# Two feed-forward blocks exchange places in a pipelined macaron kernel, with a ring of three residual buffers and a token-major beta

## What is computed

```
x = x + 0.5 * FFN(layernorm(x))          # FFN: gelu(h @ w1 + b1) @ w2 + b2, 256 -> 1024 -> 256
x = x + ATTN(layernorm(x))
x = x + 0.5 * FFN(layernorm(x))

ATTN(x): q, k, v = silu(conv4(x @ W))    # 4 heads of 64
         beta = sigmoid(x @ Wb)          # one number per token and head
         q, k = l2norm(q), l2norm(k)
         delta = delta_rule(q, k, v*beta, k*beta, chunks of 32)   # T = (I - A)^-1 per chunk
         branches = fir3(v), fir31(v), delta, v
         w = softmax(gelu([x, stats, branches] @ gW1 + gb1) @ gW2 + gb2), floored, renormalised
         return rmsnorm(sum(w * branches)) @ Wo
```

## Time and profile before

| | us |
|---|---|
| median of 3 executions (1224.04, 1224.04, 1238.88) | 1224.04 |
| the profiled execution | 1227.37 |
| its span, from the first to the last instruction | 1225.7 |
| PE busy in it | 1056.4 (86%) |
| DVE busy | 820.9 (67%) |
| ACT busy | 549.3 (45%) |
| POOL busy | 415.6 (34%) |
| mean granted TensorE clock | 0.932 of full |

### The profile page before, as it was taken

One profiled execution on the slowest core, in us unless ns is written; L12 is line 12 of the kernel. 1 busy time (PEld: TensorE's weight loads), 2 busy tenths in 40 slices (PEclk: granted clock), 3 DMA queues, 4 the chain that ended last, 5 costly groups with the idle time before them and its releaser, 6 DMA issues.

```text
span 1225.7 us, 25639 instructions
## 1 busy us (share of the span) xinstructions
PE 1056.4 (86%) x10348; PEld 784.7 (64%) x10348; DVE 820.9 (67%) x1556; ACT 549.3 (45%) x965; POOL 415.6 (34%) x648
## 2 busy tenths in 40 slices
PE   3778598899988999899988996999988998887838
PEld 2654485378745886488736884478736885477427
DVE  5774267785687767875788666875787667863263
ACT  1154236443374337543475336453475337532322
POOL 7106500671019500681028400681028400870000
PEclk9889699899999999989999999999999999995668
DMA  5040104110040203111040203011040204020000
GB/s 153 1 102 21 34 1 97 25 31 22 18 104 1 53 1 94 28 26 27 19 104 1 52 19 86 18 24 30 18 104 1 52 1 96 9 52 1 1 0 18
DMA packets 82293, 47.45 MB, mean 39 GB/s; under 512 B 57856, under 2 KB 75776, under 8 KB 82176
## 3 DMA queue, kind: packets, MB, share of 16 engines
q1 hardware_dynamic: 82176, 45.82, 16.4%
HBM read 31.12 MB, written 14.68 MB: 37 GB/s over the span
## 4 chain that ended last, share of the span: by engine, by line
PE 57%; DVE 22%; ACT 8%; issue 5%; SPq 3%; POOL 3%; DMA 1%; DVEq 0%; ACTq 0%; POOLq 0%
PE psum L782 12%; PE psum L784 10%; PE psum L783 10%; DVE conv_acc L1363 4%; PE psum L813 4%; DVE arena L1594 3%; PE psum L975 3%; PE psum L960 3%; PE psum L994 2%; PE psum L999 2%; SPq L347 2%; PE psum L1152 2%; ACT arena L582 2%; DVE arena L1596 2%; POOL arena L522 1%
## 5 line engine op out<-in xcount | busy, mean ns | idle before, releaser
L518 POOL TENSOR_TENSOR l_prod<-arena 64x30 f32<-64x30 f32 (+14 forms) x240 | 150.8, 628 | 599.2 <-DMA arena<-l_dram 581.0
L578 ACT ACTIVATE h_f<-psum,b_col 128x512 f32<-128x512 f32 x128 | 88.0, 688 | 216.4 <-PE psum L784 206.4
L522 POOL TENSOR_TENSOR arena<-arena,l_prod 64x30 f32<-64x30 f32 (+14 forms) x240 | 157.3, 655 | 18.8
L782 PE MATMUL psum<-w_hi,h_hi 128*128 128x256 f32 x512 | 152.0, 297 | 9.2 <-DVE h_lo L1343 9.2
L784 PE MATMUL psum<-w_hi,h_lo 128*128 128x256 f32 x512 | 145.2, 284 | 0.0
L783 PE MATMUL psum<-w_lo,h_hi 128*128 128x256 f32 x512 | 145.1, 283 | 0.0
L1081 PE MATMUL psum<-v_shift,fir_w 128*32 128x512 f32 x1152 | 133.6, 604 | 3.6 <-DMA v_shift<-v_dram 3.6
L1363 DVE SCALAR_TENSOR_TENSOR conv_acc<-psum,conv_col,conv_acc 128x511 f32<-128x511 f32 x144 | 107.8, 748 | 33.5 <-ACT conv_acc L603 22.4
L782 PE MATMUL psum<-xt_hi,w_hi 128*128 128x512 f32 x256 | 109.4, 427 | 14.3 <-DVE b_half L1456 7.0
L1342 DVE CAST h_hi<-h_f 128x512 fp32r<-128x512 f32 x128 | 65.3, 510 | 76.6 <-ACT h_f L578 40.1
L782 PEld LDWEIGHTS psum<-w_hi,h_hi 128*128 128x128 f32 x512 | 98.1, 192 | 15.3 <-DVE h_lo L1343 11.1
(11 more groups left out here) (232 smaller groups left out, 2205.6 us busy)
## 6 DMA issues: line engine op xcount, KB each, us to landing
x_in<-in_L_attn_x SPq DMA_DIRECT2D x8, 512.0 KB, 4.0
v_dram<-v_fm SPq DMA_DIRECT2D x8, 512.0 KB, 2.8
v_shift<-v_dram SPq DMA_DIRECT2D x8, 512.0 KB, 5.0
out<-x_tok SPq DMA_DIRECT2D x8, 512.0 KB, 2.9
v_shift<-v_dram SPq DMA_DIRECT2D x8, 511.0 KB, 7.0
v_shift<-v_dram SPq DMA_DIRECT2D x8, 510.0 KB, 9.1
v_shift<-v_dram SPq DMA_DIRECT2D x8, 509.0 KB, 11.6
arena<-in_L_ffn_w SPq DMA_DIRECT2D x2, 1024.0 KB, 7.1
```

The lines of the kernel that those rows point to most:

```text
L518: pool.tensor_tensor(prod, l_inv[:, k + 1:, k:k + 1].broadcast_to(shape), l_inv[:, k:k + 1, 0:k].broadcast_to(shape), ALU.mult).then_inc(i ...
L522: pool.tensor_tensor(l_inv[:, k + 1:, 0:k], l_inv[:, k + 1:, 0:k], prod, ALU.add).then_inc(inverted, 1)
L578: act.activation(h_f[:, m % 2, :], bank, ACT.Gelu, bias=b1_col[:, m:m + 1]).then_inc(read, 1)
L782: pe.matmul(dst, a_hi, b_hi, start=first, stop=False, **kw)
```

## The change

The wide place now runs the *first* FFN of sequence j + 1 ("upw", "outw"), and the filling place runs the *second* FFN of sequence i - 1 ("upr", "outr"). So sequence 0 still has its first FFN alone at the start; head has sequence 1's first FFN behind its front; a new pass "zero" (i = 0) has a back and a front and a wide FFN, but nothing to fill its merge and recurrence; five bodies have both; last (i = 6) fills with sequence 5's second FFN and has no wide FFN; tail fills with sequence 6's second FFN and ends with sequence 7's in the wide place. There are 16 FFNs before and after.

- Layer norm 1 of sequence j + 1 has its statistics ahead of Wo and is normalised between the two halves of Wo's reading on DVE; it is turned ("ln1") behind f_t. The first products of the wide FFN wait for each half of it apart.
- Layer norm 3 of sequence i has its statistics taken behind Wo as before, but is normalised after the fourth split of the wide FFN and turned as "next" near its end, for the filling FFN of the next pass.
- The statistics of layer norm 2 are taken at the end of a pass, behind the residual of the wide FFN, and no longer behind the recurrence.
- Rows live in x_ring, three buffers by sequence modulo 3. The copy on POOL (L499) is gone; the residuals are added in place. SP stores the output of i - 1 and then loads x of i + 2 at the start of a pass; x of sequence 1 is loaded among the weights at the start.
- at0 stands behind the first four steps of the wide FFN, and DVE masks lhalf ahead of the first split.
- beta is made by token: for each of 4 tiles and 2 halves, three products with the 128x128 block of rows as weights and 4 moving columns; ACT takes the sigmoid of 16 columns straight into rows_tok. beta_turn and the copy on DVE are gone.
- Banks: f_t moves from (0, 1, 6, 4) to (0, 1, 7, 2).

```diff
-        x_in = sb("x_in", [P, TILES, C])
-        x1_tok = sb("x1_tok", [P, TILES, C])
-        x2_tok = sb("x2_tok", [P, TILES, C])
+        x_ring = [sb(f"x_ring{n}", [P, TILES, C]) for n in range(3)]
...
+        V_T = [("v_t", (3, 5)), ("f_t", (0, 1, 7, 2))]
+        FFN_W = [("upw", (0, 4) * (KT // 2)), ("outw", (1, 6))]
...
+        front = [LN2, V, K, FIR, Q, V_T, LN1, HALF, FFN_W, L_OFF]
+        both = [STATS, LN2, V, STAT, K, LOGIT, FIR, Q, MIX, V_T]
+        ORDER = {"head": sum(front, first),
+                 "zero": sum([MERGE, RECUR] + both + [LN1, HALF, FFN_W, L_OFF, NEXT], []),
+                 "body": sum([MERGE, RECUR, FFN_R] + both + [LN1, HALF, FFN_W, L_OFF, NEXT], []),
+                 "last": sum([MERGE, RECUR, FFN_R] + both + [HALF, L_OFF, NEXT], []),
+                 "tail": sum([MERGE, RECUR, FFN_R, STATS, STAT, LOGIT, MIX, LN3, FFN_W], [])}
...
 # SP
+            load_x(1)
             sp.wait_ge(const_made, ZEROED)
...
             def one_pass(at):
+                if at.fill:
+                    store_y(at.i - 1)
+                if at.ahead and at.back:
+                    if at.fill:
+                        sp.wait_ge(y_stored, 16 * at.i)
...
+                    load_x(at.j + 1)
...
 # POOL
-                    pool.wait_ge(y_stored, 16 * at.i + 1)
-                    pool.wait_ge(x1_made, 2 * at.i + 2)
-                    pool.tensor_copy(x2_tok[:, :, :], x1_tok[:, :, :]).then_inc(x2_begun, 1)
+                if at.fill:
+                    add_bias(at.i - 1, 2, bias2_added)
...
+                if at.ahead:
+                    x_ready(pool, at.j + 1)
+                    add_bias(at.j + 1, 0, bias1_added)
...
 # ACT
-                    out_of(at, "beta", 0, beta_fm[:, :], ACT.Sigmoid, src=lambda b: b[0:32, :])
+                    out_of(at, "beta", 0, rows_tok[:, 1, :].rearrange("p (t h) -> p t h", t=TILES), ACT.Sigmoid,
...
+                if at.ahead:
+                    high(at, 0, j + 1, "ln1")
+                if at.back:
+                    root(2, i)
...
 # PE
             def beta(at):
+                for t in range(TILES):
+                    toks = slice(P * t, P * t + P)
+                    for k in range(HALVES):
+                        last = product3(pe, bank[:, 32 * t:32 * t + HEADS], xt_hi[:, k, toks], xt_lo[:, k, toks],
+                                        wb_hi[:, k, 0:HEADS], wb_lo[:, k, 0:HEADS], k == 0, k == HALVES - 1)
...
+                if at.ahead:
+                    turn_rows(at, "ln1", xn_made[0], j + 2)
+                if at.front:
                     off_diagonal(at, "lhalf")
...
+                wide(range(0, 4))
                 if at.front:
                     attend(at, 0)
+                wide(range(4, 16))
...
+                wide(range(20, 28))
+                if at.keep:
+                    turn_rows(at, "next", xn_made[2], 2 * i + 2)
+                wide(range(28, 32))
...
 # DVE
+                if at.ahead:
+                    x_ready(dve, j + 1)
+                    stats(0, rows_of(j + 1))
                 if at.back:
+                    x_seq = rows_of(i)
                     for b in range(2):
                         bank, read = arrive(dve, at, "wo", b)
...
                         dve.sem_inc(read, 1)
+                        if at.ahead and b == 0:
+                            normalise(0, j + 1, rows_of(j + 1))
...
+                if at.ahead:
+                    low(0, j + 1, "ln1")
...
+                if at.front:
+                    off_diagonal("lhalf")
+                wide_split(0)
+                wide_split(1)
...
+                wide_split(3)
+                if at.keep:
+                    normalise_out()
...
+                if at.keep:
+                    low(2, i, "next", ready=True)
+                if at.ahead:
+                    dve.wait_ge(bias1_added, j + 2)
+                    residual("outw", rows_of(j + 1), rows_of(j + 1), x1_made)
+                    stats(1, rows_of(j + 1))
```

More of the change, by code:

```diff
@@ L209, in __init__ @@
                 self.front, self.back = mode != "tail", mode != "head"
-                self.next = mode in ("head", "body")
-            def count(self, per):
-                if self.mode == "head":
-                    return 0
-                if self.mode == "body":
-                    return per("head") + self.i * per("body")
-                return per("head") + (SEQS - 2) * per("body") + (per("last") if self.mode == "tail" else 0)
+                self.fill = mode in ("body", "last", "tail")
+                self.ahead = mode in ("head", "zero", "body")
+                self.wide = self.ahead or mode == "tail"
+                self.w = self.j if self.front else i
+                self.keep = mode in ("zero", "body", "last")
+            def count(self, per):
+                before = {"head": (), "zero": ("head",), "body": ("head", "zero"), "last": ("head", "zero"),
+                          "tail": ("head", "zero", "last")}[self.mode]
+                bodies = 0 if self.i is None or self.i < 1 else min(self.i, SEQS - 2) - 1
+                return sum(per(m) for m in before) + bodies * per("body")
         def content(at, what, k):
@@ L321, in macaron_kernel @@
         T_LOADS = CPT + 2 * (CPT - 1)
-        DVE_STEPS = {"head": 49, "body": 82, "last": 77, "tail": 38}
+        DVE_STEPS = {"head": 58, "zero": 71, "body": 81, "last": 66, "tail": 48}
         CONST_MADE, C_LOADED, SETUP_DVE = 60, 57, 36
@@ L540, in one_pass @@
                     pool.wait_ge(t_zeroed, 2 * j + 2)
[L541 to L546 removed]
+                if at.ahead:
+                    x_ready(pool, at.j + 1)
+                    add_bias(at.j + 1, 0, bias1_added)
+                if not at.front:
+                    add_bias(at.i, 2, bias2_added)
             every_pass(pool, one_pass)
@@ L572, in gelu @@
             def gelu(at, f, seq, m):
-                bank, read = arrive(act, at, ("upa", "upc")[f], m)
+                bank, read = arrive(act, at, ("upr", "upw")[f], m)
                 if m >= 2:
@@ L750, in one_pass @@
                     act.sem_inc(fir_done, 1)
-                if at.next:
+                if at.ahead:
                     root(0, j + 1)
-                if at.back:
-                    root(2, i)
                 if at.front:
```

274 lines of the change are left out of this document (119 added, 155 removed).

## The result

| | before | after |
|---|---|---|
| median of 20 executions each | 1226.55 us | 1233.14 us |
| lowest to highest | 1222.41 to 1238.88 | 1228.27 to 1246.91 |
| the profiled execution, its span | 1227.37, 1225.7 | 1231.08, 1229.4 |
| mean granted clock in it | 0.932 | 0.929 |

The ratio of after to before is 1.0052, with a 95% interval of 1.0029 to 1.0075: slower by half a per cent, 6.6 us, where 3 us less had been forecast. The executions after lie in two groups, ten from 1228 to 1232 and nine from 1236 to 1247, with one between; the median of 1233.14 is the mean of the two in the middle, 1231.84 and 1234.44. A single profile shows only one of the groups, here the lower one. That turned out to be the point of this case.

A forecast was written before the change was run, and what follows sets the result against it. PE was taken as the bound in full bodies, with holes elsewhere deciding. Terms 2.9 + 1.1 - 4.2 - 1.8 - 1.1 = -3.1 us took the median from 1224.0 to 1221 us, range 1202 to 1240.

The forecast's parts named there:

- rival 5: Stalls named issue change in number with the instruction stream: 1210 us without them, 1232 with twice as many; chance 0.14.
- Head, +2.9: Head: x load's issue, beta and POOL's inversion beside DVE's splits delay the first merge by 2.9 us, to 147.2.
- Zero, +1.1 - 0.7: Pass zero: unfilled recurrence unchanged at 38 us, dense products behind it +1.1 from half clock; full-pass gain -0.7.
- Bodies, -0.7 each: Full passes: earlier wide FFN -0.3 net, DVE's beta copy gone -0.35; -0.7 us each.
- Last, -1.8: Pass last: POOL contention (1.5 us) and beta's copy (0.3) go; PE idles some 17 us for x_t.
- Tail, -1.1: Tail: filled recurrence takes 38.0 us against 38.3, and dense products behind it run warm; -1.1 us.
- 1 (layer norms in full): Every body's waits for lhalf and the low part go, 3.1 us in each of six: 1207 us; chance 0.14.
- 2 (DVE late): DVE late at a pass's start and between Wo's halves, 3.5 us in each of six passes: 1244 us; chance 0.12.
- Rival 3: Head: DVE's splits shut POOL out, costing its inversion up to 10 us instead of 1.7: 1229 us; chance 0.06.
- Rival 4: Head's wide FFN starts late or stays cold, so zero's merge starts 8 us or more later: 1229 us; chance 0.08.

The follow-up runs named there:

- e15: Kernel before, with spacer products ahead of the attention products, dealt over row and column groups: 1219.07 us, 0.9936 of the kernel before.
- e16: Changed kernel, with spacer products ahead of the attention products (9 in head, 7 in most other passes): 1216.09 us, 0.9904 of the kernel before.
- e4: Changed kernel, with layer norm 1 of the next sequence normalised ahead of Wo's loop on DVE: 1233.19 us, 1.0048 of the kernel before.
- e5: Changed kernel, with 2 Gram products repeated in head and 7 in each other pass: 1214.42 us, 0.9866 of the kernel before.
- e6: Kernel before, with 8 Gram products repeated in head and 14 in each other pass: 1237.09 us, 1.0043 of the kernel before.
- e9: Kernel before, with 31 Gram products repeated in head and 27 in three passes: 1237.43 us, 1.0092 of the kernel before.
- e3: Changed kernel, with head and the first recurrence filled as before (no wide FFN in head): 1227.02 us, 1.0005 of the kernel before.
- e14: Changed kernel, with the four copies of v issued behind the loads of the Gram blocks: 1323.28 us, 1.0763 of the kernel before.
- e12: e5 with 17 instead of 2 Gram products repeated in head: 1238.60 us, 1.0079 of the kernel before.
- e13: Kernel before, with 33 spacer products in head and 27 in three passes ahead of the attention products, results overwritten: 1223.23 us, 0.9957 of the kernel before.

## Why the prediction was wrong

The forecast was -3.1 us and the change made +6.6. The runs split this in two. Without the stalls it is -3.0 (e15 to e16), or about -2 without the spacers' share. The stalls cost 1226.6 - 1219.1 = 7 us before and 1233.1 - 1216.1 = 17 after, which is the other 10 (these are medians of different sessions; by the ratios it is 8 and 18). The step that failed is a term that isn't in the sum and so was put at nothing: the prediction held the two stalls named issue at their number and price, and gave their change only to rival 5, with 0.14 and 1232 us for twice as many. That rival is what happened, as far as the cost goes; each kernel's own profile has two such stalls, and how often there are more is not shown. Its condition, the instruction stream, was named rightly, but nothing was worked out from it. All that it needed stood in the profile: the queue of instructions with its packets, the two stalls' places just behind the Gram products, and the DMA row at 0.9 beside them. From these one can count where the pieces end, but for the one small figure that here came from several profiles. beta's 24 products in place of six and four turns (one record each) are 14 records more a pass, and shift each end.

That the pair without stalls gives just the -3.1 of the sum is luck. Head and zero cost 6.0 where 3.3 was given (2.9 + 1.1 - 0.7), and last and tail gave 6.3 where 2.9 was; the two errors nearly cancel.

That the number of stalls varies within one kernel would explain the two groups of executions. The profiles fit (after's profile has two stalls and belongs to the group of 1228 to 1232, e4's has the third and took 1240.69), but no profile of both groups of after itself was taken.

The terms, against after's profile and against the pair without stalls:

- **Head, +2.9: measured +6.9, in the pair +3.9.** The load of x was sized by the time to issue it, 0.35, but SP's issues behind it got later by more than that, and with them the landing of the last constants, for which DVE waited: 1.95 us at the projections (e16 against e15: 1.1). beta's products were sized well, 2.6 for 2.4, but in head nothing absorbs them, and the turns behind them ran at a lower clock. POOL beside the splits was right: 1.5 us for the 1.7 to 2.0. The wide FFN filled the hole.
- **Zero, +1.1 - 0.7: in the pair +2.1.** The recurrence was right, 38.16 us for 38.0 at half clock. The products behind it lost more than the 1.1 that was taken: the rest of zero takes 101.75 us, the first body's 99.84.
- **Bodies, -0.7 each: right.** 134.2 to 134.4 for the plain ones after, against 135.0, and -3.3 for five in the pair. The wait for lhalf went and f_t's took part of its place. That last wait was put at under a microsecond and is 2. e4, which takes the normalisation out of it, shortens a plain pass by 0.8.
- **Last, -1.8: measured -1.6, in the pair -3.2.** PE waits for x_t for 12.9 us ahead of tail's merge, less than the 15 to 19 named, and the inversion's stretch takes 16.2 us (1081.61 to 1097.77) where it took 17.6.
- **Tail, -1.1: measured -3.6, in the pair -3.1.** Counted from the merge, the recurrence takes 37.7 us before and 37.5 after. The part behind it takes 83.95 for 87.4, at a clock of 0.77 for 0.73; it was given 0.8 of these 3.4.

Of the rivals, 1 (layer norms in full) and 2 (DVE late) did not occur: after's bodies were neither 132 nor 138 where no stall stood. Rival 3 neither: POOL lost 1.5 us in 16 beside the splits, not 10. The prediction took the 10 from DVE's busy share. The port rule of the Trainium skill (SBUF — State Buffer, section "SBUF: two separate sides") is narrower: it names DVE instructions in a two-port mode or with two inputs in SBUF, and the lock lasts for one instruction. The trace agrees, beside the splits too. A step of POOL that runs beside a split's subtraction (L1355, two inputs) takes some 0.34 us longer, and the subtraction up to 0.98 us for 0.69. The same step before, beside nothing, and after, beside a subtraction:

```profile
128.50 0.47 POOL L522 TENSOR_TENSOR arena<-arena,l_prod 64x150 f32<-64x150 f32 x1
...
134.41 0.81 POOL L535 TENSOR_TENSOR arena<-arena,l_prod 64x150 f32<-64x150 f32 x1
```

But only six of head's 27 steps meet one, where two did before, hence 1.5 us. The steps of 2.25 us beside the mixing are still there. Rival 4 is in part the measured head, late but by 6.9 us for other reasons than the FFN.

The Trainium skill (Runtime: NRT & Kernel Launch, section "Instruction fetch mechanics") states that each engine fetches blocks of 16 KiB, 256 instructions, through a DMA queue of its own while it runs the current one, and that this is mostly hidden. The size agrees with the 16.4 KB of the packets here, and with stalls that sit 256 instructions apart or a multiple. "Mostly hidden" holds for some 80 pieces of 83. The others took 5.5 to 8.1 us each, 1 to 2% of this kernel in sum.

## What to carry to other kernels

Before a change of 1% is judged on a kernel of many small instructions, count how many instructions it adds per pass and where the pieces of 256 end. A stall named issue that sat in the middle of a group, beside a saturated DMA, was here an instruction piece that waited in line, and 14 more records a pass moved all of them. Such stalls can be removed with a few spare products, best outside the quick run: with the run lengthened to 284 instructions (e5) none was left, with 312 (e6) and 364 (e9) three stood. A comparison of two schedules means little until both are free of them. Here that was worth 17 us on the changed kernel, six times the 3 that the change itself was about.

## What the runs showed of the hardware

- PE's instructions arrive through the same DMA engines as data: 83 packets of 16.4 KB, and a stall of 5.5 to 8.1 us (once 2.8, in e3) when one is due while 2 MB of copies hold all 16 engines. It ends 1.1 to 1.6 us after the packet has landed; the packet starts 9 to 11 us after the first copy was issued (6.0 in e3's short one). With no data moving beside it, one quick run still cost a stall of 2.0 us (e14).
- It needs a quick run: 128 records in 1.29 us. In other passes a piece ends among products of 512 columns, and no stall is seen there.
- A stall is followed by a lower granted clock (0.86 in the stretch behind it in e12, 1.00 in e5), so it can cost more than its length: e12's three are 22.4 us long and cost 24. In before's profile a stall of 8.0 us cost only 4.3 (139.7 us for 135.4).
- Products of 32 columns over changing row and column groups take 10 ns a record (128 in 1.29 us); at one place, all writing the same block, 34 ns (66 in 2.27 us, e13).
- A step of POOL beside a DVE subtraction with two inputs in SBUF takes 0.34 us longer (0.81 us for 0.47), and beside products of 2.3 us it takes 2.25 us.
- 24 products with 128x128 weights and 4 moving columns take 2.6 us, 0.11 each (after).
